# Seven block products for eight of the eleven gate and up tiles of a feed-forward layer

## The reference, cut to what matters

```python
x = L0_attn_u                                  # (4, 256, 512): 1024 tokens of width 512
xn = _layernorm(x)
x = x + s4(xn) + ffn(xn)                       # layer 0
# ffn: up = xn @ W_up.T; gate = silu(xn @ W_gate.T); h = gate * up; y = h @ W_down.T      (W_*: 1376 x 512)
# s4:  K = ifft(at_roots) with Cauchy sums over 64 poles at 512 roots of unity;
#      y = causal convolution of each row of 512 with K, + D * row
xn = _layernorm(x)
x = x + attention(xn) + experts(xn)            # layer 1: 32 heads, then a gated low-rank mixture
```

## Time and profile before

| | |
|---|---|
| median of 3 runs | 1098.86 us (1098.47 to 1098.95) |
| the profiled execution, its own time | 1099.28 us |
| its span, first to last instruction | 1097.4 us |
| PE busy | 1091.9 us, 99% |
| POOL busy | 733.7 us, 67% |
| DVE busy | 698.0 us, 64% |
| ACT busy | 542.9 us, 49% |
| moved by DMA | 59.91 MB, mean 55 GB/s |

### The profile page before, as it was taken

How to read it: one execution, slowest core, us unless ns; L and a number is a source line. 1 busy time by engine, 2 the same in 40 slices (tenths; PEclk the granted TensorE clock), 3 DMA queues, 4 the chain that set the end, 5 groups by cost and what they waited for, 6 DMA issues and landing times.

```text
span 1097.4 us, 21436 instructions
## 1 busy us (share of the span) xinstructions
PE 1091.9 (99%) x6418; PEld 966.2 (88%) x6418; DVE 698.0 (64%) x1761; ACT 542.9 (49%) x1637; POOL 733.7 (67%) x988
## 2 busy tenths in 40 slices
PE   9999999999999999999999999999999999999998
PEld 8887888899998899889988988898899889988987
DVE  7554224376776666766677666766667666776675
ACT  3221132132755665556555645664565566555663
POOL 4656586797955992797299549954994599269910
PEclk9999999999999999999999999999999999999999
DMA  7213331211110120021011101110110012001102
GB/s 240 96 60 104 136 115 49 77 45 32 46 57 3 59 78 21 20 67 49 19 30 66 38 19 58 39 39 19 58 57 22 18 58 77 19 12 59 46 1 77
DMA packets 25287, 59.91 MB, mean 55 GB/s; under 512 B 3585, under 2 KB 3905, under 8 KB 25089
## 3 DMA queue, kind: packets, MB, share of 16 engines
q1 hardware_dynamic: 25216, 59.14, 16.8%
HBM read 57.03 MB, written 2.10 MB: 54 GB/s over the span
## 4 chain that ended last, share of the span: by engine, by line
PE 97%; DMA 1%; POOL 1%; issue 0%; DVE 0%; SPq 0%; ACT 0%; POOLq 0%
PE banks L181 29%; PE banks L182 29%; PE banks L183 29%; PE banks L1719 4%; PE banks L1738 3%; PE banks L1710 3%; DMA gu_stage<-in_w_gu 1%; PE banks L886 0%; PE banks L1015 0%; POOL gu_lo L367 0%; POOL gu_lo L353 0%; PE banks L924 0%; SPq L301 0%; POOL gu_hi L350 0%; PE banks L1001 0%
## 5 line engine op out<-in xcount | busy, mean ns | idle before, releaser
L1285 POOL TENSOR_TENSOR form_lo<-wqk_stage,form_hi 128x256 fp32r<-128x256 f32 x192 | 141.8, 738 | 16.0
L1339 POOL TENSOR_SCALAR vf_hi<-wvo_stage 128x512 fp32r<-128x512 f32 (+1 forms) x48 | 26.3, 548 | 176.6 <-PE banks L183 174.5
L1619 ACT ACTIVATE prob<-prob,top 128x128 f32<-128x128 f32 (+1 forms) x256 | 115.6, 460 | 17.8 <-DVE top L1648 17.6
L1625 ACT ACTIVATE prob<-prob,inv 128x128 f32<-128x128 f32 (+1 forms) x256 | 102.6, 451 | 36.1 <-DVE inv L1654 36.1
L1648 DVE CUSTOM_DVE_ANT_0 prob<-banks,mask 128x128 f32<-128x128 f32 (+1 forms) x256 | 81.3, 355 | 60.3 <-PE banks L183 45.8
L1666 DVE TENSOR_TENSOR acc<-acc,banks 128x512 f32<-128x512 f32 x128 | 86.7, 681 | 36.1 <-PE banks L183 36.0
L181 PE MATMUL banks<-tT_hi,form_hi 128*128 128x512 f32 x256 | 105.6, 412 | 0.0
L182 PE MATMUL banks<-tT_lo,form_hi 128*128 128x512 f32 x256 | 100.2, 391 | 0.0
L183 PE MATMUL banks<-tT_hi,form_lo 128*128 128x512 f32 x256 | 100.1, 391 | 0.0
L181 PE MATMUL banks<-wo_hi,oT_hi 128*128 128x512 f32 x240 | 95.9, 400 | 0.0
L183 PE MATMUL banks<-wo_hi,oT_lo 128*128 128x512 f32 x240 | 93.6, 390 | 0.0
(11 more groups left out here) (309 smaller groups left out, 3590.7 us busy)
## 6 DMA issues: line engine op xcount, KB each, us to landing
wqk_stage<-in_w_qk SPq DMA_DIRECT2D x32, 512.0 KB, 3.3
gu_stage<-in_w_gu SPq DMA_DIRECT2D x21, 512.0 KB, 3.3
wvo_stage<-in_w_v SPq DMA_DIRECT2D x34, 256.0 KB, 2.6
wvo_stage<-in_w_o SPq DMA_DIRECT2D x32, 256.0 KB, 2.7
wd_stage<-in_w_down SPq DMA_DIRECT2D x22, 256.0 KB, 2.6
acc<-in_x SPq DMA_DIRECT2D x8, 256.0 KB, 4.6
out<-acc SPq DMA_DIRECT2D x8, 256.0 KB, 2.0
tab<-in_w_comb SPq DMA_DIRECT2D x1, 1300.0 KB, 6.2
```

Of the source, the lines that this page charges most:

```text
L1285: nc.gpsimd.tensor_tensor(form_lo[:, part], src[:, :], as_f32(form_hi[:, part]), ALU.subtract).then_inc(form_ready, 1)
L1619: ins = nc.scalar.activation(pr, pr, ACT.Exp, bias=top[:, n % 2, r:r + 1], scale=-1.0, accum_out=total[:, n % 2, r:r + 1])
L1625: ins = nc.scalar.activation(pr, pr, ACT.Copy, scale=inv[:, n % 2, r:r + 1])
```

## The change

- **Tiles 0 to 2** of gate and up are made as before ("direct"), but all six (three tiles, two halves) come first. The second half of the tokens is normalised and transposed after the second of them, so that all 1024 tokens are there.
- **Tiles 3 to 10** are made once for both halves. The 2 x 2 blocks are gate and up by the two halves of the width (weights), and the halves of the width by the halves of the tokens. Seven products (P1, P2, P6, P7, P4, P5, P3) of six matmuls of 512 columns take the place of eight products of six. POOL makes four sums of weight blocks for each tile and the lo parts of seven forms, ACT the hi parts; both halves of the seven operands are held once, so a form of the next tile is written when its product of this tile is done. DVE mixes the products (seven additions for each tile) and makes h of both halves; the second half's h goes unsplit to `hF`, and is split later (`second_hi`, `second_lo`).
- **The tokens' mixed operands** `tF_hi`, `tF_lo` are made from both halves (`keep_f`, `mix_f`, `mixed_f_evac`, `mixed_lo`).
- **The state-space pieces** move: the six small pieces follow the tiles 3 to 8 on DVE, the small matmuls stand ahead of tile 9 on PE, `roots` and `phases` follow tile 10. The cosine and sine tables are loaded when the last product is done, and lie where gate and up weights had been.
- **Down**: both halves come after all gate and up tiles. `w_comb` is split between `down`'s weights of the second half.
- The gate and up weights are loaded once and not twice. Loops with registers are gone from layer 0.

The diff, cut to its core:

```diff
+    F_ORDER = P1, P2, P6, P7, P4, P5, P3
+    F_SHORT = P1, P2, P6, P7
...
+    SHORT_BANKS = D, D + 1, D + 2
...
+        for f in range(5, NF):
+            sp.wait_ge(f_ready, f_form(f - 2, BY_S4))
+            load_gu(f)
+        sp.wait_ge(f_ready, f_form(NF - 2, BY_S4))
+        for n in range(4):
+            load_wd(n)
+        sp.wait_ge(f_prod, f_product(NF - 1, P3))
+        sp.dma_start(tab[:, 0:2 * FT * DM], tables).then_inc(tab_loaded, 16)
+        sp.wait_ge(cauchy_done, 1)
         sp.dma_start(bias, b_base.partition_broadcast(P)).then_inc(bias_loaded, 16)
...
+        for n in range(4, 9):
+            load_wd(n)
+        sp.wait_ge(toep_done, 1)
+        sp.dma_start(wc_stage, w_comb.rearrange("k p n -> p k n")).then_inc(wc_loaded, 16)
+        sp.dma_start(wb_stage, w_expb).then_inc(wc_loaded, 16)
+        for n in range(9, 2 * NF):
+            load_wd(n)
 
...
+        def forms_begin(f):
+            a11, a12, a21, a22 = blocks(f)
+            pool.wait_ge(gu_loaded[f % 2], 16 * (f // 2 + 1))
+            if f > ND:
+                pool.wait_ge(f_ready, f_form(f - 1, BY_S1))
+            add(s1[:, :], a21, a22, ALU.add)
+            form_lo_part(f, BY_RAW, halves(f, 0), 0, 2)
+            pool.wait_ge(f_added, f_add(f, 1))
+            add(a21, a11, a21, ALU.subtract)
+            pool.wait_ge(f_ready, f_form(f, BY_RAW))
+            pool.wait_ge(f_added, f_add(f, 2))
+            add(a11, s1[:, :], a11, ALU.subtract)
+            pool.wait_ge(f_added, f_add(f, 3))
+            add(a12, a12, a11, ALU.subtract)
+            form_lo_part(f, BY_S2, a11.unsqueeze(1), 2, 3)
+        def forms_middle(f):
+            form_lo_part(f, BY_S3, halves(f, 1), 4, 6)
+            form_lo_part(f, BY_S1, s1[:, :].unsqueeze(1), 6, 7)
+        def forms_end(f):
+            pool.wait_ge(f_added, f_add(f, 4))
+            form_lo_part(f, BY_S4, blocks(f)[1].unsqueeze(1), 3, 4)
...
+        split_gate()
+        split_gu(0, 1)
+        split_gu(1, 0)
+        split_gu(1, 1)
+        pool.wait_ge(xn_done, NT)
+        split_gu(2, 0)
+        split_gu(2, 1)
+        forms_begin(ND)
+        mixed_lo(0)
+        mixed_lo(1)
+        forms_middle(ND)
+        mixed_lo(2)
+        mixed_lo(3)
+        forms_end(ND)
+        for f in range(ND + 1, NF):
+            forms_begin(f)
+            forms_middle(f)
+            forms_end(f)
+        for n in range(MASK_AFTER + 1):
+            split_wd(n)
+        pool.wait_ge(toep_copied, 1)
+        nc.gpsimd.affine_select(out=s4[:, 5, 0:P], in_=s4[:, 5, 0:P], compare_op=ALU.is_ge, fill=0.0,
+                                base=0, pattern=[[1, P]], channel_multiplier=-1).then_inc(toep_masked, 1)
+        for n in range(MASK_AFTER + 1, NF + 2):
+            split_wd(n)
+        pool.wait_ge(wc_loaded, 32)
+        split_comb(0)
+        split_comb(1)
+        split_wd(NF + 2)
+        split_comb(2)
+        split_wd(NF + 3)
+        split_comb(3)
+        for n in range(NF + 4, 2 * NF):
+            split_wd(n)
...
+        def f_tile(f):
+            following = f + 1 if f + 1 < NF else None
+            copy_p1(f)
+            if following:
+                form_hi_part(following, BY_RAW)
+            f_silu_half(f, 0)
+            if following:
+                form_hi_part(following, BY_S2)
+                form_hi_part(following, BY_S3)
+            h_hi(f, f_bank(f, P4))
+            if following:
+                form_hi_part(following, BY_S1)
+                form_hi_part(following, BY_S4)
+            f_silu_half(f, 1)
...
+        def second_hi(chunks):
+            for c in chunks:
+                act.wait_ge(g_done, NF)
+                act.wait_ge(wd_used, c + 1)
+                nc.scalar.activation(hT_hi[:, c], hF[:, c], ACT.Copy).then_inc(h_hi_done, 1)
 
...
+        silu_direct(5)
+        for f in range(ND, NF):
+            f_tile(f)
+            if f == ND + 3:
+                squares()
+        second_hi(range(0, 4))
         act.wait_ge(toep_ready, 1)
         nc.scalar.activation(toep_hi[:, :], s4[:, 6, :], ACT.Copy).then_inc(toep_ready, 1)
-        ffn(1)
+        second_hi(range(4, NF))
         sqrt_var(2)
         for t in range(TH):
...
+        def f_tile(f):
+            bank = {i: banks[:, f_bank(f, i)] for i in F_ORDER}
+            dve.wait_ge(f_prod, f_product(f, P2))
+            dve.wait_ge(f_copied, f - ND + 1)
+            nc.vector.tensor_tensor(bank[P2], p1, bank[P2], ALU.add).then_inc(f_mix, 1)
+            dve.wait_ge(f_prod, f_product(f, P6))
+            nc.vector.tensor_tensor(u2, p1, bank[P6], ALU.add).then_inc(f_mix, 1)
+            dve.wait_ge(f_prod, f_product(f, P7))
+            dve.wait_ge(f_mix, f_mixes(f, F_U2))
+            nc.vector.tensor_tensor(u3, u2, bank[P7], ALU.add).then_inc(f_mix, 1)
+            dve.wait_ge(f_prod, f_product(f, P4))
+            dve.wait_ge(f_mix, f_mixes(f, F_U3))
+            nc.vector.tensor_tensor(bank[P4], u3, bank[P4], ALU.add).then_inc(f_mix, 1)
+            dve.wait_ge(f_mix, f_mixes(f, F_C21))
+            h_first(f, silu_1, f_silu(f, 0), f_bank(f, P4))
+            dve.wait_ge(f_prod, f_product(f, P5))
+            nc.vector.tensor_tensor(u2, u2, bank[P5], ALU.add).then_inc(f_mix, 1)
+            nc.vector.tensor_tensor(bank[P5], u3, bank[P5], ALU.add).then_inc(f_mix, 1)
+            dve.wait_ge(f_prod, f_product(f, P3))
+            dve.wait_ge(f_mix, f_mixes(f, F_U4))
+            nc.vector.tensor_tensor(bank[P3], u2, bank[P3], ALU.add).then_inc(f_mix, 1)
+            h_lo(f, f_bank(f, P4))
+            dve.wait_ge(f_mix, f_mixes(f, F_C22))
+            h_second(f, silu_2, f_silu(f, 1), f_bank(f, P5))
+        def second_lo(chunks):
+            for c in chunks:
+                dve.wait_ge(h_hi_done, NF + c + 1)
+                nc.vector.tensor_tensor(hT_lo[:, c], hF[:, c], as_f32(hT_hi[:, c]), ALU.subtract).then_inc(h_lo_done, 1)
 
...
+        load_stats(range(TH, NT))
+        variance(range(TH, NT))
+        for t in range(TH):
+            keep_f(t)
+        inverse_deviation(1, range(TH, NT))
+        normalise(range(TH, NT))
+        direct_first(0)
+        direct_lo(0)
+        direct_first(1)
+        for t in range(TH, TH + 2):
+            xT_evac(t, D + t - TH)
+        direct_lo(1)
+        for t in range(TH + 2, NT):
+            xT_evac(t, D + t - TH)
+        mix_f(0)
+        direct_first(2)
+        mix_f(1)
+        direct_lo(2)
+        mix_f(2)
+        direct_second(3)
+        mix_f(3)
+        direct_second(4)
+        direct_second(5)
+        def small_vectors():
+            input_weights()
+            step_size()
+        pieces = [small_vectors, cauchy_real, cauchy_imag, cauchy_numerators, cauchy_reciprocal, cauchy_inverse]
+        for f in range(ND, NF):
+            f_tile(f)
+            if f - ND < len(pieces):
+                pieces[f - ND]()
+        roots(0)
+        roots(1)
         phases()
-        for t in range(TH, NT):
-            xT_evac(t, G + t - TH)
+        second_lo(range(0, 4))
         toeplitz()
+        second_lo(range(4, NF))
...
+        def f_tile(f):
+            for i in F_ORDER:
+                right, k0, half = {P1: ((xT_hi, xT_lo), 0, 0), P6: ((tF_hi, tF_lo), FT, 0), P2: ((xT_hi, xT_lo), FT, 0),
+                                   P7: ((tF_hi, tF_lo), 2 * FT, 0), P4: ((tF_hi, tF_lo), 0, 0),
+                                   P5: ((tF_hi, tF_lo), 3 * FT, 0), P3: ((xT_hi, xT_lo), FT, 1)}[i]
+                cols = slice(half * HALF, (half + 1) * HALF)
+                bank = f_bank(f, i)
+                f_wait(f, i)
+                at = F_PLACE[i]
+                for c in range(FT):
+                    ins = matmul3(nc, banks[:, bank], form_hi[:, at, c], form_lo[:, at, c],
+                                  right[0][:, k0 + c, cols], right[1][:, k0 + c, cols],
+                                  c == 0, c == FT - 1)
+                ins.then_inc(f_prod, 1)
 
...
+        direct_tile(1)
+        for t in range(TH, NT):
+            if t == TH:
+                pe.wait_ge(xT_kept, TH)
+                pe.wait_ge(f_kept, TH)
+            transposes(t, D + t - TH)
+        for n in range(2, 2 * ND):
+            direct_tile(n)
+        for f in range(ND, NF):
+            if f == ND + 6:
+                pe.wait_ge(cauchy_in, 1)
+                for t in range(KD):
+                    out = banks[:, G + 3, 8 * t:8 * t + 8]
+                    nc.tensor.matmul(out, dr[:, t * P:(t + 1) * P], vv[:, 0:8], start=True, stop=False)
+                    ins = nc.tensor.matmul(out, di[:, t * P:(t + 1) * P], vv[:, 8:16], start=False, stop=True)
+                ins.then_inc(cauchy_done, 1)
+            f_tile(f)
+        pe.wait_ge(f_mix, f_mixes(NF - 1, F_U3))
+        pe.wait_ge(silu_done, f_silu(NF - 1, 0))
+        down(0, range(0, 5))
         pe.wait_ge(cauchy_read, 1)
...
         pe.wait_ge(uv_done, 1)
         for i, table in enumerate((cos_t, sin_t)):
             for t in range(FT):
```

(46 more changed lines are left out.)

436 lines of the change are left out of this document (272 added, 164 removed).

## The result

The changed kernel takes 1104.23 us (median of 5 runs, 1103.84 to 1105.09) against 1098.86 us for the kernel before (5 runs, 1098.47 to 1099.12): **ratio 1.0051 [1.0036, 1.0066]**, 5.4 us slower. The forecast was 1103.6 us. The profiled execution took 1104.64 us with a span of 1102.9 us; the span before was 1097.4 us.

What follows compares the result with a forecast made beforehand. PE's issue of matmuls, busy 99% of the span, was taken as the bound. Terms summed to +4.7 on the profiled 1099.28 us, 1104.0, less 0.42 for the median: 1103.6 us, range 1095.5 to 1107.5.

Steps and rivals of the forecast that it cites:

- eight tiles of block products: Tiles 3 to 10 on PE: 42 matmuls take 9.59 us in place of 10.88, -10.4 us (bounds -10.9 and -8.7).
- the early wait: PE's one real wait in layer 0 goes, as the second token half gives POOL time: -0.5 us (0 to -0.5).
- gap ahead of tile 9: PE's small matmuls wait for `cauchy_in` from DVE, which comes late to tile 8: +4.6 us (3.5 to 5.5).
- half clock behind it: After each of two PE gaps, 4 to 5 us of work at half rate: +2.2 us each, 4.4 us (0 to 5.4).
- gap ahead of the tables: After five `down` chunks PE waits for `uv_done`, DVE's roots being held up by POOL's splits: +3.9 us (0 to 5.5).
- `w_comb` between the splits: Second half's `down`: two `w_comb` pieces between POOL's splits make PE wait, +2.7 us.
- POOL late once in the first half's `down`: No such wait was forecast; the later h splits `second_hi` and `second_lo` under `down` were put at nothing.
- Do the others keep up: At 9.6 us a tile, POOL (8.1), DVE (7.0) and ACT (5.4 us) all fit: cost 0, bounds up to 3 us.
- Second fall of the clock: PE's clock falls 2 us into its idle wait for `uv_done`, then half rate costs +2.2 us.
- the gaps without the clock: Rival: the clock stays up, or only one gap is long; 1099.2 us with both gaps, chance 0.22.
- The free roots: Rival: DVE's short chains slip between POOL's operations, `uv_done` comes in time, the clock holds; 1095.3 us, chance 0.18.
- The fourth: Rival: DVE or POOL can't hold the pace of block products or mixed tokens; 1106 to 1109 us, chance 0.15.

Runs made afterwards that it cites:

- e8_pool_held: Changed kernel with POOL's third split for `down` waiting for `uv_done`, so POOL stands still while DVE makes roots and phases; 1110.11 us in one run.
- e1_sums_later: Changed kernel with the pole sums one tile later on PE, ahead of tile 10; 1095.65 us, ratio 0.9962 to the kernel before.
- e7_gap_filled_more: Changed kernel with 23 unread products of zeros (46 passes) on PE ahead of the wait for `cauchy_in`, which stays; 1100.82 us, ratio 1.0011 to the kernel before.
- e3_tables_later: Changed kernel with the product with the cosine and sine tables behind seven chunks of `down`, not five; 1099.09 us, ratio 0.9998 to the kernel before.
- e2_comb_order: Changed kernel with three pieces of `w_comb` split under the first convolve and the fourth behind `down`'s last split; 1101.59 us, ratio 1.0018 to the kernel before.
- e6_roots_earlier: Changed kernel with `roots(0)` on DVE behind its part of tile 9, not tile 10; 1100.25 us, ratio 1.0012 to the kernel before.
- e5_gap_filled: Changed kernel with 19 unread products of zeros (38 passes) on PE ahead of the wait for `cauchy_in`, which stays; 1102.16 us, ratio 1.0023 to the kernel before.

## Why the prediction was right

It gave 1103.6 us and "slower" at 0.60; the median is 1104.2. Its terms, each beside what PE's starts show in the two traces:

| step | predicted | measured |
|---|---|---|
| eight tiles of block products | -10.4 | -10.9 |
| the early wait | -0.5 | -0.5 |
| gap ahead of tile 9 | +4.6 | +5.0 |
| half clock behind it | +2.2 | +4.0 |
| gap ahead of the tables | +3.9 | +3.1 |
| half clock behind it | +2.2 | +1.8 |
| `w_comb` between the splits | +2.7 | +3.2 |
| POOL late once in the first half's `down` | 0 | +0.3 |
| sum | +4.7 | +6.0 |

Against this sum, the product with `w_comb`, which follows on layer 0's last convolution, starts 5.6 us later (217.12 before, 222.72 after), and the first tile 0.2 us earlier (12.72, 12.48): 5.8 us lie between. The rows of the table are good to some tenths.

- **Block products**: a tile takes 9.52 us, the bound without any price for a change between products (10.88 - 9.52 = 1.36, x 8). The other bound, a late start for each product, did not come.
- **Do the others keep up**: they do. Between tiles 3 and 9 no wait of PE appears, although DVE ran its pieces there.
- **First gap**: the mechanism is the one described; the timeline of DVE below has the reciprocal behind tile 7, the last mix of tile 8, its `h_second`, and L925, which ended at 109.36 us; PE started at 109.42. The step that was too small is the clock. I had put the fall at 4 to 5 us of work at half rate, from the start of the kernel; that half clock was read from the pace of the matmuls alone (11 and 20 in 2 us), for both windows list a granted clock of 1.00. The rows above show half clock from 107.7 to 117.7: pole sums of 3.5 us in place of 1.9, then twelve matmuls in 5.1 us in place of 2.7. Behind a gap of 7.5 us in e8_pool_held, where PE goes on with matmuls of 512 columns alone, the half clock took 4.9 us of work (147.59 to 152.5), the size that I had put. Whether the sixteen matmuls of 8 columns at the start of the work made the difference was not tested by itself.
- **Second gap**: roots stood under POOL's splits and took 9.0 us. With POOL held they take 4.8 us, so the cause is shown and not only argued. I had them end 13.5 us behind tile 10 where they ended 11.5 behind (134.42 to 145.96), and the phases at 16.6, not 17.5. Three operations of the roots took 1.1 us or more, one in each 2.72 us of POOL's (at 138.25, 140.96 and 143.81); I had stepped through four such periods.
- **Second fall of the clock**: it came, but not by the step that I gave (a fall 2 us into the gap). The clock was still at 1.00 in the gap's last stretch and fell at 152 us, after PE had started again. Behind the same gap it did not fall in every execution: the mean granted clock is 1.000 in one of six runs of e1_sums_later and in four of ten of e7_gap_filled_more. So this term came true partly by luck.
- **`w_comb`**: 1.3 + 1.9 us, 0.5 more than predicted.
- **Small miss**: the tenth chunk of the first half's `down` started 0.3 us late. Its weights are queued on SyncE behind `toep_done` and the loads of `w_comb`, so POOL waited for the DMA; and its lo part took 1.60 us, not the usual 1.30, beside DVE's `second_lo`, which I had put at nothing. The rows are below. In e3_tables_later the load is issued earlier and POOL's lo part still takes 1.60 us, but PE's wait is gone. As far as the two traces show, the load was the part that counted.

The timeline of DVE of the changed kernel, for the first gap:

```profile
97.91 3.35 DVE L920 RECIPROCAL s<-s 64x512 f32<-64x512 f32 x1
...
106.00 0.69 DVE L856 TENSOR_TENSOR banks<-sums,banks 128x512 f32<-128x512 f32 x1
...
107.49 0.69 DVE L799 TENSOR_TENSOR hF<-banks,work 128x512 f32<-128x512 f32 x1 [0.20 <-ACT work L613]
...
108.69 0.67 DVE L925 SCALAR_TENSOR_TENSOR s<-banks,s 64x512 f32<-64x512 f32 x1
```

The timeline of POOL of the changed kernel, for the small miss:

```profile
165.05 0.77 POOL L478 TENSOR_SCALAR wd_hi<-wd_stage 128x512 fp32r<-128x512 f32 x1 [0.86 <-DMA wd_stage<-in_w_down]
165.90 1.60 POOL L480 TENSOR_TENSOR wd_lo<-wd_stage,wd_hi 128x512 fp32r<-128x512 f32 x1
```

The Trainium skill (SBUF — State Buffer, Who interferes with whom) says that a DVE instruction with two SBUF inputs contends with a GpSimd instruction that reads SBUF, through a shared port that one of them holds alone. The traces agree where they were put to the test: 4.8 us became 9.0 us, and an operation of four columns became 1.26 us long, ending within 0.03 us of POOL's beside it.

Of the rivals, the gaps without the clock (1099.2 us) is refuted by the windows, and its size by e7_gap_filled_more: holding the clock at the first gap alone gave back 3.3 to 3.6 us. The free roots (1095.3 us) are refuted by the chain of 9.0 us; e8_pool_held shows what they would be. The fourth, DVE or POOL too slow for the tiles, has no wait that speaks for it.

The prediction was close partly by luck: its largest misses are +1.8 us (the first half clock) and -0.8 us (the second gap), and with the smaller ones they offset each other in part; the terms measured add up to 1.3 us more than those forecast, while the median came 0.6 us above the forecast. What carried it were the three waits read out of the order of the code.

## What to carry to other kernels

Where one engine is busy 99% of the time, a scheme that saves its work is worth its count of instructions, and each wait that the new order puts in front of it is paid in full, a long one then again by the clock: here 5.0 us of waiting cost 9, while waits of 1.3 and 1.9 us cost no more than their length. Ask, for each small piece that such an engine must run, when its input is ready and how many tiles later it could be had for nothing; moving the piece by one tile, two chunks and one place made a change that was 5.4 us slower 10.7 us faster. On an in-order engine that lacks time, look at what its neighbour does on the same memory before counting its instructions: 38 small operations took 9.0 or 4.8 us by that alone.

## What the runs showed of the hardware that I had not expected

- Behind the same gap of 5.0 us, with the same code on PE up to there, the granted clock fell and came back at different times in the profiled executions of five kernels. It was at 0.50 from 107.6 to 117.9 in the changed kernel, and for as long in e2_comb_order and e8_pool_held (10.2 us), but only from 108.9 to 115.7 in e3_tables_later and from 109.0 to 115.9 in e6_roots_earlier (6.8 us). PE's work began at 109.2 to 109.5 in all of them.
- A gap of 3.1 us left the clock at 1.00 while PE was idle (window 148.2 to 151.0); it fell to 0.50 about 1 us after PE had started again, under matmuls of 512 columns, and stayed there for 3.4 us. In the profiled execution of e7_gap_filled_more the same gap had the fall inside it, 0.3 us ahead of PE's start, and in four of that kernel's ten runs the mean granted clock shows no fall at all.
- Sixteen matmuls of 8 columns behind a wait of 0.6 us did not keep the clock: it fell in tile 9 (e5_gap_filled). With no wait left ahead of them it stayed at 1.00 (e7_gap_filled_more), and so it did in e1_sums_later, where they stand between full tiles. The runs agree: eight of ten of e5_gap_filled have a mean granted clock of 0.997, and none of e7_gap_filled_more is under 0.998. What exactly tips it was not measured.
- Matmuls of 128 columns whose result nobody reads held the clock at 1.00 through a gap: 23 fp32 products, 46 passes, gave back 3.3 to 3.6 us.
- The hold-up was seen on both sides. Four columns on DVE took 1.26 us in place of 0.16 beside POOL's lo part; POOL's lo part took 1.60 us in place of 1.30 beside DVE's `second_lo`, which no edit tested by itself.
